# Causal mask of the transposed scores: an identity matmul on TensorE in place of selects on GpSimd

## The reference

```python
h = _layernorm(x) * (1 + ca) + sa
q = h @ w_dq.T @ w_uq.T                    # 16 heads of 16
k, v = split(h @ w_dkv.T @ w_ukv.T)
attn = einsum('bhqd,bhkd->bhqk', q, k) * SCALE
attn = attn + triu(full((s, s), -inf), k=1)   # causal mask
attn = softmax(attn, axis=-1)
x = x + ga * (einsum('bhqk,bhkd->bhqd', attn, v) @ w_out.T)
h = _layernorm(x) * (1 + cb) + sb
x = x + gb * ffn(h)     # two experts: gelu and relu, hidden 512 each, chosen per token by argmax
```

## Time and profile before

| | before |
|---|---|
| three runs | 622.82, 625.32, 628.98 us |
| median | 625.32 us |
| span of the profiled execution | 624.9 us |
| mean granted TensorE clock | 0.939 of full speed |
| busy ACT | 364.2 us, 58% of the span |
| DMA | 43.74 MB, 70 GB/s on average |
| POOL affine selects of `hide`, L1246 | 96 |
| POOL affine selects of `hide_scores`, L1235 | 96 |

### The profile page before, as it was taken

The page is one execution under the profiler, slowest core; times in us unless marked ns, Lnnn a source line. Parts: engine busy times, 40 slices in busy tenths (PEclk is TensorE's granted clock), DMA queues, the critical chain, the costliest instruction groups (busy, mean ns, idle before and its releaser), DMA issues.

```text
span 624.9 us, 14082 instructions
## 1 busy us (share of the span) xinstructions
PE 510.3 (82%) x4720; PEld 434.0 (69%) x4720; DVE 489.5 (78%) x949; ACT 364.2 (58%) x521; POOL 387.6 (62%) x393
## 2 busy tenths in 40 slices
PE   5635675988888988999888888788898888989974
PEld 4424454786776878787868777687777786868873
DVE  3438254779797977999798988798997979898564
ACT  2424553857574764767575767566576757575420
POOL 5135443758585776776685858667676768575551
PEclk9956596899999997999999999999999999999998
DMA  8644253331615070514325160606143241501000
GB/s 255 159 58 68 35 73 68 63 76 38 117 27 129 1 153 3 101 53 70 83 47 106 25 127 11 142 0 128 24 90 65 60 95 38 100 3 37 35 18 17
DMA packets 43802, 43.74 MB, mean 70 GB/s; under 512 B 5344, under 2 KB 40800, under 8 KB 43760
## 3 DMA queue, kind: packets, MB, share of 16 engines
q1 hardware_dynamic: 43760, 43.19, 34.3%
HBM read 13.39 MB, written 4.23 MB: 28 GB/s over the span
## 4 chain that ended last, share of the span: by engine, by line
DVE 33%; PE 18%; issue 16%; DMA 14%; SPq 8%; POOL 5%; ACT 3%; DVEq 1%; POOLq 0%; ACTq 0%
DMA xs<-x 9%; DVE mx L928 9%; SPq L281 7%; DVE z L867 4%; POOL xs L1175 4%; DVE y L966 3%; DVE hid L1074 3%; PE ps_s L381 3%; DMA qs<-parts_q 2%; DMA qs<-mx_rows 2%; ACT score_rows L789 2%; DVE hid_hi L1087 2%; DVE y L962 2%; DVE parts_q L985 2%; PE ps_c L332 1%
## 5 line engine op out<-in xcount | busy, mean ns | idle before, releaser
L789 ACT ACTIVATE score_rows<-ps_s 128x1024 f32<-128x1024 f32 x96 | 98.9, 1030 | 98.1 <-PE ps_s L381 66.6
L928 DVE TENSOR_REDUCE mx<-score_rows 128x4 f32<-128x1024 f32 (+1 forms) x96 | 114.0, 1208 | 6.4 <-POOL score_rows L1235 6.4
L1235 POOL TENSOR_SCALAR_AFFINE_SELECT score_rows<-score_rows 128x512 f32<-128x512 f32 (+1 forms) x96 | 80.4, 838 | 49.3 <-ACT score_rows L789 49.3
L801 ACT ACTIVATE p<-ps_t 128x1024 f32<-128x1024 f32 x96 | 98.9, 1030 | 15.0 <-PE ps_t L399 14.8
L1246 POOL TENSOR_SCALAR_AFFINE_SELECT p<-p 128x512 f32<-128x512 f32 (+1 forms) x96 | 81.1, 845 | 20.2 <-ACT p L801 20.1
L381 PE MATMUL ps_s<-ks,qs 96*128 96x256 bf16 (+1 forms) x512 | 65.8, 268 | 23.0 <-DMA qs<-parts_q 17.3
L399 PE MATMUL ps_t<-qs,ks 99*128 99x256 bf16 (+1 forms) x512 | 62.8, 259 | 24.6 <-DMA qs<-mx_rows 23.0
L381 PEld LDWEIGHTS ps_s<-ks,qs 96*128 96x128 bf16 x512 | 38.4, 106 | 36.9 <-DMA qs<-parts_q 18.0
L851 DVE BATCH_NORM_STATS2 ln_st<-xs 128x6 f32<-128x256 f32 (+1 forms) x64 | 24.0, 417 | 49.9 <-DMA xs<-x 36.1
L399 PEld LDWEIGHTS ps_t<-qs,ks 99*128 99x128 bf16 x512 | 39.1, 103 | 33.4 <-DMA qs<-mx_rows 17.4
L1175 POOL TENSOR_TENSOR xs<-z,xs 128x512 f32<-128x512 f32 (+1 forms) x16 | 33.4, 2090 | 39.8 <-DVE z L1017 39.7
(11 more groups left out here) (162 smaller groups left out, 1660.8 us busy)
## 6 DMA issues: line engine op xcount, KB each, us to landing
qs<-parts_q SPq DMA_DIRECT2D x96, 128.0 KB, 3.6
ks<-parts_k SPq DMA_DIRECT2D x96, 128.0 KB, 4.5
xs<-x SPq DMA_DIRECT2D x16, 256.0 KB, 5.0
gates<-gates_scratch SPq DMA_DIRECT2D x16, 256.0 KB, 4.3
out<-xs SPq DMA_DIRECT2D x16, 256.0 KB, 4.0
p<-wmod SPq DMA_DIRECT2D x1, 1024.0 KB, 6.3
p<-waT SPq DMA_DIRECT2D x1, 1024.0 KB, 8.9
p<-wmod SPq DMA_DIRECT2D x1, 512.0 KB, 5.4
```

What stands on the lines that cost most here:

```text
L789: act.activation(score_rows[c % 2][:], ps_s[:], ACT.Copy).then_inc(scores_out, 1)
L801: act.activation((p0, p1)[tile][:, h0:h0 + n, :], ps_t[:].rearrange("p (h s) -> p h s", h=n), ACT.Exp, scale=SCALE).then_inc(exp_done, 1)
L928: dve.tensor_reduce(dst, score_rows[c % 2][:].rearrange("p (h k) -> p h k", h=n), AX_X, ALU.max).then_inc(max_done, 1)
L1235: pool.affine_select(out=diag, in_=diag, compare_op=ALU.is_ge, fill=NEG, base=0, pattern=[[0, n], [-1, P]], channel_multiplier=1).then_inc ...
```

## The change

`hide` and its semaphore `masked` are taken out. At the start POOL builds a second constant: `past`, a 128 x 128 tile with zero where the query (column) is not earlier than the key (row) and -3e38 where it is, copied to bf16 as `past_b`. In `st_chunk` the heads' matmuls no longer close their sums; the first in a bank clears the bank's flags, and when all are issued, two more matmuls, one for each bank, multiply the bf16 identity by `past_b`, repeated over the heads of that bank, and add the result to the diagonal blocks. For tile 0 such a matmul covers two heads (256 columns, the blocks 256 apart), for tile 1 four heads (512 columns). The exponential of the sum is then zero where the mask stands. `values` waits for `exp_done` in place of `masked`. PE's first wait for constants asks for six in place of three.

```diff
--- before.py
+++ after.py
@@ -103,6 +103,7 @@
         bias_b = sb("bias_b", [P, 2 * D])
         ident = sb("ident", [P, P])
         ident_b = sb("ident_b", [P, P], BF16)
+        past_b = sb("past_b", [P, P], BF16)
         neg_half = sb("neg_half", [P, TT])
         modT = sb("modT", [P, NB, 8])
 
@@ -158,6 +159,7 @@
         wb_raw = [hid32[:].rearrange("p a b s -> p (a b) s"), oT[:]]
         wdq_raw, wuq_raw, wuv_raw, wg_raw = z2[:], attn[:], score_rows[0][:, 0:D], logits[:]
         cT_raw, c_silu = mx[:], mx_rest[:]
+        past = y[:, 0, 0:P]
         clamped, sign = [g[:].rearrange("p g d -> p (g d)")[0:NB] for g in gates]
 
 
@@ -177,8 +179,7 @@
             "ckv_done ckv_hi_ready ckv_ready v_done v_ready".split())
         s_done, scores_out, scores_hidden, max_done, max_split, mt_done = (sem(n) for n in
             "s_done scores_out scores_hidden max_done max_split mt_done".split())
-        mt_ready, st_done, exp_done, masked, pv_done, o_ready = (sem(n) for n in
-            "mt_ready st_done exp_done masked pv_done o_ready".split())
+        mt_ready, st_done, exp_done, pv_done, o_ready = (sem(n) for n in "mt_ready st_done exp_done pv_done o_ready".split())
         ot_done, rden_ready, attn_ready, at_done, a_hi_ready, a_lo_ready, op_done, gated_ready, x1_ready = (sem(n) for n in
             "ot_done rden_ready attn_ready at_done a_hi_ready a_lo_ready op_done gated_ready x1_ready".split())
         z2_ready, t2_done, g32_ready, g_hi_ready, g_lo_ready = (sem(n) for n in
@@ -395,9 +396,13 @@
                 wait(pe, exp_done, CH * b.n + c)
                 tile, h0, n = ST[c]
                 width = S - P * tile
+                a_bank = 512 // width
                 for h in range(n):
-                    mm = pe.matmul(ps_t[:, h * width:(h + 1) * width], ks[b.parity][0:RM, h0 + h, tile * P:(tile + 1) * P],
-                                   qs[b.parity][0:RM, h0 + h, tile * P:S], start=True, stop=True)
+                    pe.matmul(ps_t[:, h * width:(h + 1) * width], ks[b.parity][0:RM, h0 + h, tile * P:(tile + 1) * P],
+                              qs[b.parity][0:RM, h0 + h, tile * P:S], start=h % a_bank == 0, stop=False)
+                for bank in range(2):
+                    diag = ps_t[:, bank * 512:(bank + 1) * 512].rearrange("p (h q) -> p h q", h=a_bank)[:, :, 0:P]
+                    mm = pe.matmul(diag, ident_b[:], past_b[:].unsqueeze(1).to_broadcast([P, a_bank, P]), start=False, stop=True)
                 mm.then_inc(st_done, 1)
 
             def values(b, g, *users):
@@ -406,7 +411,7 @@
                     return
                 if g == 0:
                     pe.wait_ge(v_ready, b.n + 1)
-                pe.wait_ge(masked, CH * b.n + ST_OF_GROUP[g])
+                pe.wait_ge(exp_done, CH * b.n + ST_OF_GROUP[g])
                 bank_left(users)
                 for n in range(4):
                     h = 4 * g + n
@@ -595,7 +600,7 @@
                                    start=k == 0, stop=k == 1)
             mm.then_inc(wq_done, 1)
 
-            pe.wait_ge(consts_ready, 3)
+            pe.wait_ge(consts_ready, 6)
             pe.wait_ge(blank, 4)
             pe.wait_ge(z1_ready, 1)
             turn(BANK["T1"], z1, t1_done)
@@ -1154,6 +1159,12 @@
                                pattern=[[-1, P]], channel_multiplier=1).then_inc(consts_ready, 1)
             pool.wait_ge(consts_ready, 2)
             pool.tensor_copy(ident_b[:], ident[:]).then_inc(consts_ready, 1)
+            pool.memset(past, 0.0).then_inc(consts_ready, 1)
+            pool.wait_ge(consts_ready, 4)
+            pool.affine_select(out=past, in_=past, compare_op=ALU.is_ge, fill=NEG, base=0,
+                               pattern=[[1, P]], channel_multiplier=-1).then_inc(consts_ready, 1)
+            pool.wait_ge(consts_ready, 5)
+            pool.tensor_copy(past_b[:], past).then_inc(consts_ready, 1)
 
             def inverse_deviation(b, n):
 
@@ -1235,18 +1246,6 @@
                 pool.affine_select(out=diag, in_=diag, compare_op=ALU.is_ge, fill=NEG, base=0,
                                    pattern=[[0, n], [-1, P]], channel_multiplier=1).then_inc(scores_hidden, 1)
 
-            def hide(b, c):
-
-                if b.off:
-                    return
-                tile, h0, n = ST[c]
-                pool.wait_ge(exp_done, CH * b.n + c + 1)
-                wait_alone(pool)
-                diag = (p0, p1)[tile][:, h0:h0 + n, 0:P]
-                pool.affine_select(out=diag, in_=diag, compare_op=ALU.is_ge, fill=0.0, base=0,
-                                   pattern=[[0, n], [1, P]], channel_multiplier=-1).then_inc(masked, 1)
-
-
             pool.wait_ge(blank, 1)
             inverse_deviation(Batch(0, 0, NB), 0)
 
@@ -1263,21 +1262,15 @@
             def step(at):
                 hidden_low(at(4), 1)
                 first_inverse(at(0))
-                hide(at(2), 0)
                 add_attn(at(3))
                 hide_scores(at(1), 0)
                 inverse_deviation(at(3), 1)
                 hide_scores(at(1), 1)
                 h_low(at(0))
-                hide(at(2), 1)
                 hide_scores(at(1), 2)
-                hide(at(2), 2)
                 hide_scores(at(1), 3)
-                hide(at(2), 3)
                 g_low(at(3))
-                hide(at(2), 4)
                 hide_scores(at(1), 4)
-                hide(at(2), 5)
                 hide_scores(at(1), 5)
                 gate_ffn(at(4))
                 add_ffn(at(4))
```

## The result

| | before | after | ratio of after to before, 95% |
|---|---|---|---|
| median of the runs | 625.14 us (4 runs) | 599.99 us (4 runs, 598.75 to 604.47) | 0.9616 (0.9555 to 0.9677) |
| the same kernels, another chip | 626.55 us (7 runs) | 605.35 us (4 runs) | 0.9658 (0.9598 to 0.9719) |
| profiled span | 624.9 us | 599.3 us (second trace: 604.5) | |

The changed kernel is about 4% faster. I had said 618.5 with a range of 604 to 633: the sign was right, the size that I had said was a quarter of the measured one, and the median lies outside the range.

The account below looks back on a forecast made before the run. It took a ring of DVE work, SP's queue and the x load as the bound, PE becoming next: 12.4 steps x -0.8 = -9.9, fill +2, drain +1.2, together -6.7 us, giving 618.5 us, range 604 to 633.

Parts of the forecast that it names:

- DVE's ring: Loop from x load through DVE's work to `q_second`'s cast, then SP and next x load; 1.5 to 1.8 us a step shorter.
- The cause of the shorter casts: On DVE: removing POOL's select after exponential 0 (`hide(at(2), 0)`) would cut the `hidden_high` cast from 1.04 to 0.40 us.
- Price of the masks: On PE: the 12 added matmuls, 4096 columns a batch, would cost 1.75 us a batch.
- C: Rival on PE: repeated operand or gapped output at half pace, 3.5 us a batch, 641 us in all; chance 0.09.
- D: Rival on PE: the mask matmuls' weight loads exposed, 2.95 us a batch, 633 us in all; chance 0.07.
- PE's room: PE's idle time ahead of DVE results, 2.7 us a step, less 1.75 for masks leaves 0.95, capping the step's gain.
- the 1.0 us before `st_chunk` 0: PE's wait per step for the maxima's DMA, taken as latency started by PE's own `turn_maxima`, so no slack.
- The sign that I had named for PE as the bound: In the loop, PE's waits for DVE would fall from 2.7 us a step to almost none.
- rival A: DVE sets the pace and PE has room: the step loses the whole 1.7 us, 607 us in all; chance 0.17.
- Fill: From 40 to 136 us, at lower clock: added PE work would cost +2 us, bounds -1 and +5.8.
- Drain: Last batch's score chunks, in the chain themselves: masks would cost +1.2 us, bounds 0 and 1.75.
- The range: Whole kernel: 604 to 633 us, from the case of PE having room to that of exposed weight loads.

Follow-up runs that it names:

- e10b: The kernel before, with SP issuing the x load first in its step instead of seventh behind the stacks: 607.34 us, ratio 0.9727.
- e2: The changed kernel with all six POOL selects a batch put back and `values` waiting for `masked`, so both ways of masking at once: 617.62 us, ratio 0.9845.
- e14: The kernel before with all its selects, plus mask matmul pairs on PE in chunks 1 to 5 but not 0: 616.55 us, ratio 0.9850.
- e15: The kernel before with all its selects, plus mask matmul pairs on PE in chunks 3 to 5 only: 613.36 us, ratio 0.9804.
- e3a: The changed kernel with the three selects after exponentials 0, 1 and 3 put back, `values` waiting for them: 613.47 us, ratio 0.9773.
- e1: The kernel before without its six selects a batch and no masks instead, `values` waiting for `exp_done`: 603.19 us, ratio 0.9602.
- e5: The changed kernel with its mask matmuls issued twice, 24 a batch: 617.65 us, ratio 0.9838, step 33.07 us.
- e5b: The changed kernel with its mask matmuls issued three times, 36 a batch: 639.62 us, ratio 1.0224, step 34.85 us.
- e12: The changed kernel with the x load first on SP, and POOL's `gate_ffn` and `add_ffn` moved behind `q_third` and DVE's split of the maxima: 608.01 us, ratio 0.9709.

## Why the prediction was wrong, step by step

- **DVE's ring, 1.5 to 1.8 us a step shorter.** Near. Its work fell by 24.6 - 22.4 = 2.2 us: 0.5 before the first `normalise`, 0.3 at the second, 0.8 behind it, and 0.4 at `q_second`, which I had counted as zero. The ring itself (cast, SP's queue, x load, DVE) was right for the kernel before, as e10b shows. In the changed kernel `add_ffn` on POOL is in it as well, through `load_gates`.
- **The cause of the shorter casts.** Wrong in part. I gave the cast of `hidden_high` to the removal of select 0. Runs e2, e14, e15 and e3a have it short in the loop with select 0 in place: the order of the queues decides. Over half of the 2.05 us a step comes with the masks' delay of PE alone (34.02 to 32.86, e2), the rest from the selects that went. Without masks (e1) the missing selects alone gave 32.38, so the two are not a sum.
- **Price of the masks.** Right, 1.74 us against 1.75. Rivals C and D fell with it.
- **PE's room: this is the step that failed.** I wrote "2.7 - 1.75 = 0.95 us a step. That is below DVE's 1.5 to 1.8, so PE becomes the bound". I had counted only PE's waits for DVE, and set the 1.0 us before `st_chunk` 0 aside as latency of a ring that PE itself starts, and had left out the waits that the view puts down to "issue". By e5 and e5b the room was 4.4, so 2.6 were left after the masks, more than DVE's 2.05, and DVE kept the pace. Of the 1.7 that I had missed, some 0.3 is in the wait for the maxima: it fell from 1.0 us a step to 0.2 in the changed kernel, but was 0.7 again in e5 and e5b, where PE has no room left. The weight loads' waits down to "issue" at L332, 1.0 us a step before, are gone in e5 and e5b; that they are the greater part of the rest is likely and not shown. The sign that I had named for PE as the bound, its waits for DVE going to almost none, came true for the three that I had counted (19.0 us in seven steps before, 1.0 between 272 and 485 us after), although PE was not the bound. That makes rival A the right one, at 607 for a step of -1.7; I gave it 0.17.
- **Fill, +2.** Wrong in sign or zero: -0.2 between like starts, and hidden under 7 us of chance. **Drain, +1.2.** -0.7 in one trace and +0.9 (126.1 against 125.2 us from the last x load to the end) in the other: zero within that.
- **The range.** Its low end came from A alone with fill and drain paid on top; without those 3 us A is at 604, and with the measured 2.05 us a step in place of 1.7 it is at 625 - 12.4 x 2.05 = 599.6. The changed kernel gave 599.99 on one chip and 605.35 on another, to either side of that end, and its two traces, 599.3 and 604.5, differ by the start. So it is partly chance on which side of 604 the median fell; that the step fell by 2.05 and not by 0.8 is not.

## What to carry to other kernels

Before calling an engine the next bound, measure its ring: add a known cost to it twice, and see at which step the time begins to grow by all of it. Idle time read from an engine's waits can be too low: here 2.7 us were read and 4.4 measured. Where a queue issues a load that needs nothing behind work that is late, put it first: one moved line was worth 2.7% here, over two thirds of what the whole change brought. Before moving work to a later place, look at what a queue holds behind it, as `load_gates` held the maxima in e12. And where two engines stretch each other's instructions, look for races that a tenth of a microsecond decides: any change to one engine's timing can flip them.

## What was not expected of the hardware

A kernel got 1.5% faster (0.9845, 0.9806 to 0.9883) by 192 added matmuls with nothing removed, through the order in which POOL and DVE instructions started (0.17 us ahead against 0.13 behind). A vector instruction on 128 x 32 elements, `mx_rest`, took 1.1 us beside POOL's work and 0.19 us without it. And two traces of one kernel differed by 7.1 us at the x load at 117 us, with the same matmuls at 1.71 and 3.23 us, as the granted clock rose at 15.2 us in one and at 23.8 us in the other; that is as large as the effect that I had predicted.
